# Gated cross attention with a routed feed-forward layer: queries kept on chip, gate on VectorE, new instruction orders

## The chip, the cores and the metric

The kernel runs on one core of one Trainium2 chip. The time is the device time of one execution in microseconds; lower is better. Before the change the median of three runs is 403.4 us (403.11 to 404.89).

## The reference, cut to what matters

`x` is 8 batches of 256 tokens of 256 features in float32, the context is 8 batches of 77 keys of 192 features, and there are 16 heads of 16 features.

```python
q = layernorm(x) @ wq + bq;  k = y @ wk + bk;  v = y @ wv + bv     # 16 heads of 16
attn = softmax(q k^T / sqrt(16))                                  # 256 x 77 per head and batch
x = x + tanh(g_xattn) * ((attn v) @ wo + bo)
z = layernorm(x)
top1 = argmax(softmax(z @ gate_w.T))                              # 2 experts
routed = sum over experts e of  relu(mask_e(z) @ w1[e] + b1[e]) @ w2[e] + b2[e]
shared = relu(z @ sw1 + sb1) @ sw2 + sb2                          # hidden size 1024
x = x + tanh(g_ffn) * (routed + shared)
```

The expert that a token did not choose sees a zero row, so it adds the constant row `relu(b1[e]) @ w2[e]`, called the other row below.

## The kernel before, in words

Most matrix products are made in float32r from a high and a low part of each operand: a helper `cut` issues three products (high·high, low·high, high·low). The attention values and the transposes are float32.

The work falls into a start (context turned, keys, values, first normalisation), attention over batches 0 to 7, the shared layer over five units (batches [0], [1,2], [3,4], [5,6], [7]) which is woven into the attention, and a routed loop over nine tiles of 256 sorted tokens. For the shared layer each unit has eight hidden chunks `h.u.c` and eight output chunks `y.u.c`. The gate and the counting of a unit (`ga`, `gt`, `ct`, then `ch`, `pl` on VectorE) give each token its slot; `scat` writes its row there by an indirect DMA, and the loop reads the sorted rows.

Every engine runs its own list of steps in a fixed order, written out as a string (`PE_ORDER`, `ACT_ORDER`, `DVE_ORDER`, `POOL_ORDER`, `SP_ORDER`, lines 73 to 139); semaphores join them. A step is `name.batch.part`. One batch of attention is: `nm` normalise (ScalarE), `in` turn the rows (TensorE), `ine`/`inl` cut them into high and low parts (ScalarE, VectorE), `qy` queries (TensorE), four quarters of scores `sc` (TensorE, L1452), each with maximum `sm`, subtraction `ss` and sum `su` (VectorE, L1144 to L1169), exponential `ex` (ScalarE) and division `di` (GpSimd, L672), then five turns `tn`, attend `va`, projection `ou` (TensorE) and the residual `x1` (VectorE).

From batch 1 on the queries go round through DRAM. ScalarE writes them twice, as float32 (`q32`) and rounded (`qe`, L849), GpSimd makes the low part (`ql`, L661), SyncE stores both parts (`qw`, L460) and loads them back as four pieces into `q_stack` (`qr`, L470), where one column block of 128 rows holds two heads four times. Keys go the same way (`kw`, `kr`, L434, L444: eight loads for each batch) and so do the values (`vw`, `vr`, L482, L496). All of these DMAs stand in SyncE's one list, and each of its waits holds back what stands behind it. Scores of one quarter are four products of 154 columns. All quarters use one pair of PSUM banks, `s_ps`, so quarter k+1 waits until VectorE has subtracted quarter k.

`LO_ON_POOL` (L71) names the hidden chunks whose low part GpSimd makes instead of VectorE. The gate is made of cut products on TensorE and turned back; the other rows are 48 products with a broadcast stationary operand (L1585).

## Time and profile before

| | |
|---|---|
| median of three runs | 403.4 us |
| the profiled execution | 406.97 us |
| its span, first to last instruction | 405.2 us |
| TensorE busy | 347.0 us (86%) |
| VectorE busy | 238.9 us (59%) |
| ScalarE busy | 211.7 us (52%) |
| GpSimd busy | 168.3 us (42%) |
| mean granted TensorE clock | 0.948 of full |

The span is what the trace covers; the execution's own time is 1.8 us longer. Busy shares are averages over stages that have different limits, so the windows below are cut where the first quarter of scores of each batch starts on TensorE: 31.44 us for batch 0, 53.23, 75.45, 103.60, 123.88, 143.90, 164.13 and 184.40 us for batches 1 to 7, and 286.48 us for the first product of the routed loop. In the names of operands, `q_parts`, `q_dram`, `q_stack` are the queries' round trip; `A<-B,C` is output and inputs.

### The profile page before, as it was taken

The page shows a single profiled execution, that of the slowest core. Times are in us where ns is not written, and L with a number is a line of the kernel's source. Part 1 is how long each engine was busy: PE and PEld are TensorE (multiplying, and loading weights), DVE is VectorE, ACT ScalarE, POOL GpSimd, SP SyncE. Part 2 cuts the span into 40 slices and gives each one's busy share as a digit, 9 for nine tenths or more (in the row PEclk, how much of TensorE's full clock was granted, in tenths as well). Part 3 has the DMA queues.
Part 4 walks back from the last instruction along what each step waited for, and adds up shares of the span by engine and source line. Part 5 has one row for each costly group of instructions (what it writes and reads, how often), then busy time and mean ns, then how long its engine had stood idle before and what let it go on. Part 6 is the DMA issues. An engine that isn't in the chain of part 4 may idle for free.

```text
span 405.2 us, 7324 instructions
## 1 busy us (share of the span) xinstructions
PE 347.0 (86%) x2411; PEld 317.5 (78%) x2411; DVE 238.9 (59%) x528; ACT 211.7 (52%) x430; POOL 168.3 (42%) x185
## 2 busy tenths in 40 slices
PE   1886637939799999999999999798799999999990
PEld 0664536828798889998899978688799999999990
DVE  4697639647689888787884248442244443444440
ACT  2538737244456667536485254633455566456450
POOL 9196825423162446232430118121234554544451
PEclk9999956978899999999999999899899999999995
DMA  6946898999979293703042011002202222111120
GB/s 183 326 107 141 208 302 208 284 236 169 214 138 200 79 205 110 141 11 106 21 144 98 2 52 54 0 26 79 79 7 73 78 78 68 42 48 42 62 78 26
DMA packets 49823, 45.82 MB, mean 113 GB/s; under 512 B 20942, under 2 KB 41973, under 8 KB 49797
## 3 DMA queue, kind: packets, MB, share of 16 engines
q1 hardware_dynamic: 46114, 37.90, 37.9%
q0 software_dynamic: 2784, 6.91, 5.4%
q10 hardware_dynamic: 899, 0.69, 0.6%
q8 instruction: 14, 0.23, 0.3%
q14 instruction: 12, 0.10, 0.1%
HBM read 29.98 MB, written 16.02 MB: 114 GB/s over the span
## 4 chain that ended last, share of the span: by engine, by line
PE 59%; DVE 12%; SPq 11%; DMA 8%; issue 4%; ACT 2%; POOL 1%; ACTq 1%; DVEq 0%; POOLq 0%
PE y_ps L1365 20%; PE h_ps L1365 15%; PE bank L1365 11%; PE s_ps L1365 9%; SPq L455 4%; DMA k_stack<-k_dram 2%; SPq L477 2%; SPq L493 2%; PE bank L1483 2%; DMA vec_rows<-in_L_ffn_gate_w 2%; DMA q_dram<-q_parts 2%; DVE nt L1049 2%; DVE rsum L1165 1%; DMA xs<-sorted_dram 1%; DVE probs L1159 1%
## 5 line engine op out<-in xcount | busy, mean ns | idle before, releaser
L676 POOL TENSOR_TENSOR probs<-probs,rinv 128x616 f32<-128x616 f32 x32 | 38.9, 1220 | 65.0 <-DVE rinv L1169 65.0
L1331 DVE TENSOR_TENSOR hT_lo<-h,hT_hi 128x256 fp32r<-128x256 f32 x72 | 33.6, 466 | 49.0 <-ACT h L1025 44.3
L1022 ACT ACTIVATE hT_hi<-h_ps,vec_cols 128x256 fp32r<-128x256 f32 x36 | 17.1, 476 | 47.3 <-PE h_ps L1365 43.9
L1365 PE MATMUL y_ps<-ew_hi,hT_hi 128*128 128x256 f32 x144 | 41.7, 289 | 0.0
L934 ACT ACTIVATE hT_hi<-h_ps,vec_cols 128x512 fp32r<-128x512 f32 (+1 forms) x40 | 24.1, 602 | 31.7 <-PE h_ps L1365 31.2
L1365 PE MATMUL y_ps<-ew_hi,hT_lo 128*128 128x256 f32 x144 | 40.5, 281 | 0.0
L1365 PE MATMUL y_ps<-ew_lo,hT_hi 128*128 128x256 f32 x144 | 40.5, 281 | 0.0
L1365 PE MATMUL bank<-pT,v_diag 128*128 128x256 f32 (+1 forms) x160 | 38.5, 397 | 0.3 <-DVE place_int L1231 0.3
L1365 PE MATMUL y_ps<-sw_hi,hT_hi 128*128 128x256 f32 x128 | 37.9, 296 | 0.9 <-DVE x_all L1259 0.9
L1483 PE MATMUL bank<-ident,probs 128*128 128x128 f32 (+1 forms) x160 | 24.9, 287 | 13.7 <-ACT q_parts L861 10.7
L1365 PE MATMUL y_ps<-sw_hi,hT_lo 128*128 128x256 f32 x128 | 36.1, 282 | 0.0
L1365 PE MATMUL y_ps<-sw_lo,hT_hi 128*128 128x256 f32 x128 | 36.1, 282 | 0.0
L1365 PEld LDWEIGHTS bank<-pT,v_diag 128*128 128x128 f32 (+1 forms) x160 | 31.5, 201 | 5.0 <-DVE place_int L1231 0.5
L766 POOL DMA_INDIRECT out<-final,scatter_token x18 | 20.3, 1125 | 34.5 <-issue 21.6
L1147 DVE TENSOR_REDUCE smax<-s_ps 128x8 f32<-128x616 f32 x32 | 24.9, 779 | 13.3 <-PE s_ps L1365 13.3
L1365 PE MATMUL h_ps<-x2T_hi,sw_hi 128*128 128x512 f32 (+1 forms) x80 | 30.1, 376 | 3.0 <-ACT h L939 3.0
L1483 PEld LDWEIGHTS bank<-ident,probs 128*128 128x128 f32 (+1 forms) x160 | 18.8, 144 | 17.0 <-ACT q_parts L861 11.6
L704 POOL TENSOR_TENSOR hT_lo<-h,hT_hi 128x512 fp32r<-128x512 f32 (+1 forms) x10 | 10.7, 1067 | 50.3 <-ACT h L939 50.3
L868 ACT ACTIVATE probs<-probs 128x616 f32<-128x616 f32 x32 | 23.0, 717 | 15.2 <-DVE probs L1159 15.2
L1165 DVE TENSOR_REDUCE rsum<-probs 128x8 f32<-128x616 f32 x32 | 25.2, 789 | 7.9 <-ACT probs L868 7.8
L1250 DVE TENSOR_TENSOR hT_lo<-h,hT_hi 128x512 fp32r<-128x512 f32 (+1 forms) x30 | 19.3, 647 | 16.9 <-ACT h L939 16.5
L1365 PE MATMUL h_ps<-x2T_lo,sw_hi 128*128 128x512 f32 (+1 forms) x80 | 28.4, 355 | 0.0
(186 smaller groups left out, 1107.6 us busy)
## 6 DMA issues: line engine op xcount, KB each, us to landing
q_stack<-q_dram SPq DMA_DIRECT2D x28, 256.0 KB, 5.6
v_diag<-v_rows SPq DMA_DIRECT2D x8, 512.0 KB
stage<-in_L_ffn_w SPq DMA_DIRECT2D x4, 1024.0 KB, 7.0
q_dram<-q_parts SPq DMA_DIRECT2D x7, 512.0 KB, 3.4
sorted_dram<-empty_rows SPq DMA_DIRECT2D x10, 257.0 KB, 10.7
xs<-sorted_dram SPq DMA_DIRECT2D x10, 257.0 KB
k_stack<-k_dram SPq DMA_DIRECT2D x56, 38.5 KB, 4.7
stage<-in_L_ffn_sw SPq DMA_DIRECT2D x2, 1024.0 KB, 9.1
```

The costliest lines, as they stand in the source:

```text
L455: sp.dma_start(k_stack[to, n, :, :, h, :].rearrange("r i g n -> r (i g) n").bitcast(F32), k_dram[h * HEAD_DIM:(h + 1) * HEAD_DIM, piece // ...
L676: nc.gpsimd.tensor_tensor(pq, pq, rinv[:, b % 2, k, :].unsqueeze(2).to_broadcast([P, HG, KEYS]), ALU.mult).then_inc(p_ready, 1)
L766: pool.indirect_dma_start(out=out[:, :], out_offset=bass.IndirectOffsetOnAxis(ap=scatter_token[:, t:t + 1], axis=0), in_=final[:, t, :], i ...
L868: nc.scalar.activation(probs[:, b % 2, k, :], probs[:, b % 2, k, :], ACT.Exp, scale=HEAD_DIM ** -0.5).then_inc(p_exp, 1)
L934: nc.scalar.activation(hT[0][:, q % HB, 0:width], h_ps[:, q % 2, 0:width], ACT.Relu, bias=b1_sb[:, 0, c:c + 1]).then_inc(h_hi, 1)
L1022: nc.scalar.activation(hT[0][:, c % HB, 0:RTOK], hidden_bank(c % 4)[:, 0:RTOK], ACT.Relu, bias=b1_sb[:, 1 + e, c:c + 1]).then_inc(h_hi, 1)
L1147: nc.vector.tensor_reduce(out=smax[:, b % 2, k, :].rearrange("p (n h) -> p n h", n=2), in_=score_heads(), axis=AX_X, op=ALU.max).then_inc( ...
L1165: nc.vector.tensor_reduce(out=rsum[:, b % 2, k, :], in_=probs[:, b % 2, k, :].rearrange("p (h k) -> p h k", k=KEYS), axis=AX_X, op=ALU.add ...
L1250: nc.vector.tensor_tensor(hT[1][:, q % HB, 0:width], h32[:, q % 2, 0:width], hT[0][:, q % HB, 0:width], ALU.subtract).then_inc(h_lo, 1)
L1331: nc.vector.tensor_tensor(hT[1][:, c % HB, 0:RTOK], h32[:, c % 2, 0:RTOK], hT[0][:, c % HB, 0:RTOK], ALU.subtract).then_inc(h_lo, 1)
L1365: return nc.tensor.matmul(out_, lhsT, rhs, start=start, stop=stop, **kw)
L1483: ins = nc.tensor.transpose(bank[m][0:ROWS[c], v * SEQ + t * P:v * SEQ + (t + 1) * P], probs[:, b % 2, g * TB + t, c * P:c * P + ROWS[c]], ...
```

## The change

- Queries no longer pass through DRAM. For each half of 64 rows (four heads) of a group, `q_stack` holds the high part in its own 64 rows and the low part in the other 64. ScalarE writes `q32` from PSUM and then copies the two halves (`qe`); GpSimd makes the low part in two instructions of 64 rows each, with a drain before and after each.
- Keys are laid out to match: `k_hi2` has the high part in both halves, over four heads, and `k_lo1` the low part. A batch takes 16 loads instead of 8, each of 16 rows with 4 or 2 pieces; the stores are 4 DMAs in place of 8 for each half of the batches. Scores of a quarter are four products of 308 columns, two over 128 rows and two over 64 rows.
- Quarters 0 to 7 (batches 0 and 1) alternate between `s_ps` and `h_ps`; values in the start go through `y_ps` instead of `h_ps`.
- The gate is one multiply with accumulation on VectorE per tile of 128 tokens; `ga`, `gt` and their ScalarE copies are gone. The other rows are eight multiply-adds on VectorE per expert and one float32 product with `ones`.
- Loads: the bias rows go on SyncE's queue right behind the first tile of x and the gate's row on GpSimd's; the big load of x waits for the second tile; the zero fill of the sorted rows (`fl`, ten DMAs) stands first in SyncE's list instead of behind the loads of batch 2. `k_hi2` is cleared on VectorE at its start.
- Statistics of batches 2 to 7 are taken batch by batch; `LO_ON_POOL` has five chunks of eight; the last weight split is on VectorE; the wait for the shared layer's last sum moves behind the first hidden products of the loop, and the loop's count is read on TensorE at `xst`. All five orders are new. `warm` issues nothing (`WARM = 0`).

```diff
@@ constants and orders (the order strings are cut)
-LO_ON_POOL = (0, 7)
+LO_ON_POOL = (2, 3, 4, 5, 7)
+WARM = 0
...
+    warm vt yt.0 yt.1 yt.2 yt.3 kp.0.0 kp.0.1 kp.1.0 in.0.0 kp.1.1 qy.0.1 vp.0 sc.0.0 sc.0.1 vp.1 in.1.0 vp.2
+    vp.3 sc.0.2 qy.1.1 sc.0.3 tn.0.0.0 tn.0.1.1 tn.0.2.0 tn.0.3.1 tn.0.4.0 in.2.1 sc.1.0 sc.1.1 qy.2.0 in.3.1
+    sc.1.2 sc.1.3 va.0.0 qy.3.1 sc.2.0 ou.0.0 in.4.1 sc.2.1 tn.1.0.0 tn.1.1.1 qy.4.0 tn.1.2.1 sc.2.2 tn.1.3.0
+    tn.1.4.1 in.5.0 sc.2.3 va.1.1 tn.2.0.0 sc.3.0 tn.2.1.0 ou.1.1 qy.5.0 sc.3.1 tn.2.2.1 tn.2.3.0 tn.2.4.1
...
+    fl vz kw.1 kw.0 wd.0 vw.0 kr.1 wd.1 vw.1 vr.0 kr.2 vw.2 vr.1 wd.2 kr.3 vw.3 vr.2 kr.4 vw.4 vr.3 wd.3 vw.5
+    vr.4 kr.5 vw.6 vr.5 kr.6 vw.7 ps.0 vr.6 kr.7 ps.1 vr.7 wd.4 wd.5 ps.2 xs ps.3 ps.4
...
-        q_stack = sb("q_stack", [P, 2, STACKS, GROUPS, SEQ], F32R, scope=att)
-        k_stack = sb("k_stack", [P, 2, STACKS, GROUPS, 2, KEYS], F32R, scope=att)
-        q_parts = sb("q_parts", [P, 2, GROUPS, SEQ], F32R, scope=att)
+        q_stack = sb("q_stack", [P, 2, GROUPS, 2, SEQ], F32R, scope=att)
+        k_hi2 = sb("k_hi2", [P, 2, 2 * GROUPS, HH, KEYS], F32R, scope=att)
+        k_lo1 = sb("k_lo1", [P, 2, GROUPS, HH, KEYS], F32R, scope=att)
         q32 = sb("q32", [P, GROUPS, SEQ], scope=att)
...
+        def score_banks(quarter):
+
+            return h_ps if quarter < 8 and quarter % 2 else s_ps
...
+            at = 0
+            for vec in (bq, bk, sb1, b1.rearrange("e h -> (e h)")):
+                n = vec.shape[0] // P
+                sp.dma_start(vec_rows[at:at + n, :], vec.rearrange("(n p) -> n p", p=P)).then_inc(vecs_in, 16)
+                at += n
...
+            sp.wait_ge(x_in[1], 16)
...
             def keys_in(b):
 
                 n = b % 2
-                if b == 1:
+                if b <= 2:
                     sp.wait_ge(cleared[0], 1)
+                    sp.wait_ge(cleared[1], 1)
                 else:
                     sp.wait_ge(s_ready, 4 * (b - 1))
-                sp.wait_ge(k_out[b // 4], 16 * 2 * STACKS)
-                for piece in range(4):
-                    for h in range(2):
-                        to = slice(piece * SR + h * HEAD_DIM, piece * SR + (h + 1) * HEAD_DIM)
-                        sp.dma_start(k_stack[to, n, :, :, h, :].rearrange("r i g n -> r (i g) n").bitcast(F32),
-                                     k_dram[h * HEAD_DIM:(h + 1) * HEAD_DIM, piece // 2, :, :,
-                                            b * KEYS:(b + 1) * KEYS].rearrange("r i g n -> r (i g) n")
+                sp.wait_ge(k_out[b // 4], 16 * 4)
+                cols = slice(b * KEYS, (b + 1) * KEYS)
+                for h in range(HH):
+                    rows = slice(h * HEAD_DIM, (h + 1) * HEAD_DIM)
+                    for m in range(2):
+                        to = slice(m * HR + h * HEAD_DIM, m * HR + (h + 1) * HEAD_DIM)
+                        sp.dma_start(k_hi2[to, n, :, h, :].bitcast(F32),
+                                     k_dram[0, :, rows, cols].rearrange("c r n -> r c n")).then_inc(k_in[n], 16)
+                        sp.dma_start(k_lo1[to, n, :, h, :].bitcast(F32),
+                                     k_dram[1, m * GROUPS:(m + 1) * GROUPS, rows, cols].rearrange("c r n -> r c n")
                                      ).then_inc(k_in[n], 16)
-
-            def queries_out(b):
-
-                sp.wait_ge(q_hi, b + 1)
-                sp.wait_ge(q_lo, b)
-                if b >= 3:
-                    sp.wait_ge(q_in[b % 2], 16 * 4 * ((b - 1) // 2))
-                sp.dma_start(q_dram[b % 2].rearrange("m p g s -> p m (g s)"),
-                             q_parts[:, :, :, :].rearrange("p m g s -> p m (g s)").bitcast(F32)
-                             ).then_inc(q_out[b % 2], 16)
-
-            def queries_in(b):
-
-                n = b % 2
-                if b >= 2:
-                    sp.wait_ge(s_ready, 4 * (b - 1))
-                sp.wait_ge(q_out[n], 16 * ((b + 1) // 2))
-                for piece in range(4):
-                    sp.dma_start(q_stack[piece * SR:(piece + 1) * SR, n, :, :, :].rearrange("r i g s -> r i (g s)"
-                                                                                            ).bitcast(F32),
-                                 q_dram[n, piece % 2].rearrange("(i r) g s -> r i (g s)", i=STACKS)
-                                 ).then_inc(q_in[n], 16)
...
             def queries_lo(b):
 
-                pool.wait_ge(q_32, b)
                 pool.wait_ge(q_hi, b + 1)
-                if b >= 2:
-                    pool.wait_ge(q_out[(b - 1) % 2], 16 * (b // 2))
-                nc.gpsimd.tensor_tensor(q_parts[:, 1, :, :].rearrange("p g s -> p (g s)"),
-                                        q32[:, :, :].rearrange("p g s -> p (g s)"),
-                                        q_parts[:, 0, :, :].rearrange("p g s -> p (g s)"), ALU.subtract
-                                        ).then_inc(q_lo, 1)
+                pool.drain()
+                for h in range(2):
+                    rows, other = slice(h * HR, (h + 1) * HR), slice((1 - h) * HR, (2 - h) * HR)
+                    ins = nc.gpsimd.tensor_tensor(q_stack[other, b % 2, :, h, :], q32[rows, :, :],
+                                                  q_stack[rows, b % 2, :, h, :], ALU.subtract)
+                    pool.drain()
+                ins.then_inc(q_lo, 1)
...
-                nc.gpsimd.tensor_tensor(lo, stage[:, n % 2, :], hi, ALU.subtract).then_inc(w_lo[n], 1)
+                for piece in range(4):
+                    cols = slice(piece * PTOK, (piece + 1) * PTOK)
+                    ins = nc.gpsimd.tensor_tensor(lo[:, cols], stage[:, n % 2, cols], hi[:, cols], ALU.subtract)
+                ins.then_inc(w_lo[n], 1)
...
+                ins.then_inc(q_32 if b else q_hi, 1)
+
+            def queries_hi(b):
+
+                act.wait_ge(q_32, b)
+                if b >= 3:
+                    act.wait_ge(s_ready, 4 * (b - 1))
+                for h in range(2):
+                    rows = slice(h * HR, (h + 1) * HR)
+                    ins = nc.scalar.activation(q_stack[rows, b % 2, :, h, :], q32[rows, :, :], ACT.Copy)
+                ins.then_inc(q_hi, 1)
...
+            def gate_difference():
+
+                dve.wait_ge(gate_in, 16)
+                nc.vector.tensor_tensor(gate_diff[:, :], gate_rows[:, 1, :], gate_rows[:, 0, :], ALU.subtract
+                                        ).then_inc(gate_cut, 1)
...
+            def other_sums(e, part):
+
+                n = 3 + 2 * e
+                w2_in = stage[:, n % 2, :].rearrange("p (c d) -> p c d", c=HC)
+                dve.wait_ge(w_in[n], 16)
+                dve.wait_ge(rb_cut, 1)
+                for c in range(part * HB, (part + 1) * HB):
+                    scale = relu_b1[:, e, c:c + 1]
+                    if c == 0:
+                        nc.vector.tensor_scalar(other_sum[:, e, :], w2_in[:, c, :], scale, None, ALU.mult
+                                                ).then_inc(other_step[e], 1)
+                        continue
+                    dve.wait_ge(other_step[e], c)
+                    nc.vector.scalar_tensor_tensor(out=other_sum[:, e, :], in0=w2_in[:, c, :], scalar=scale,
+                                                   in1=other_sum[:, e, :], op0=ALU.mult, op1=ALU.add
+                                                   ).then_inc(other_step[e], 1)
...
+                dve.wait_ge(gate_cut, 1)
+                dve.wait_ge(xn2_ready, u + 1)
+                for t in range(tiles):
+                    ins = nc.vector.scalar_tensor_tensor(
+                        out=gate_term[:, t, :], in0=xn2[:, u % 2, t, 0:DIM], scalar=1.0, in1=gate_diff[:, :], op0=ALU.mult,
+                        op1=ALU.mult, accum_out=gate_sb[:, t:t + 1])
+                ins.then_inc(gate_rdy, 1)
...
-                        pe.wait_ge(q_in[b % 2], 16 * 4 * ((b + 1) // 2))
-                        pe.wait_ge(k_in[b % 2], 16 * 8 * ((b + 1) // 2))
-                    for i in range(STACKS):
-                        ins = mm(s_ps[:, i // 2, i % 2 * SK:(i % 2 + 1) * SK],
-                                 q_stack[:, b % 2, i, g, t * P:(t + 1) * P],
-                                 k_stack[:, b % 2, i, g, :, :].rearrange("p h k -> p (h k)"), True, True)
+                        pe.wait_ge(q_lo, b)
+                        pe.wait_ge(k_in[b % 2], 16 * 16 * ((b + 1) // 2))
+                    tokens = slice(t * P, (t + 1) * P)
+                    for half in range(2):
+                        mm(s_to[:, half, 0:HALF], q_stack[:, b % 2, g, half, tokens],
+                           k_hi2[:, b % 2, half * GROUPS + g, :, :].rearrange("p h k -> p (h k)"), True, False)
+                    for half in range(2):
+                        rows = slice(half * HR, (half + 1) * HR)
+                        ins = mm(s_to[:, half, 0:HALF], q_stack[rows, b % 2, g, half, tokens],
...
+            def other(m):
+
+                fill_bank(m, other_scaled, 1)
+                pe.wait_ge(iotas, 8)
+                for e in range(EXPERTS):
+                    pe.wait_ge(other_step[e], HC)
+                    ins = mm(bank[m][:, e * DIM:(e + 1) * DIM], ones[:, :], other_sum[:, e, :], True, True)
...
+                    pe.wait_ge(seam_rdy, 1)
+                    tiles_of_0 = pe.value_load(tiles0_int[0:1, 0:1], min_val=1, max_val=RTILES - 1)
...
-            pe.wait_ge(y_out, len(UNITS))
```

## Rows read from the trace of the kernel before

**Rows 1.** Ten windows; us, then busy us per engine, PEclk, DMA share, GB/s.

```profile
0.00:31.44 31.44, 19.27 (x86) 13.72 (x86) 22.34 (x74) 12.33 (x27) 21.33 (x42) 1.00 0.71 204
31.44:53.23 21.79, 12.32 (x72) 9.19 (x73) 13.05 (x27) 14.42 (x30) 15.57 (x18) 0.98 0.78 185
53.23:75.45 22.22, 15.85 (x68) 13.86 (x69) 14.88 (x18) 11.86 (x20) 10.88 (x9) 0.64 0.93 272
75.45:103.60 28.15, 17.94 (x114) 15.78 (x112) 19.47 (x45) 11.87 (x24) 7.01 (x7) 0.88 0.99 197
103.60:123.88 20.28, 20.28 (x141) 19.38 (x141) 14.98 (x27) 12.10 (x26) 8.24 (x8) 0.92 0.88 211
123.88:143.90 20.02, 18.90 (x129) 16.38 (x128) 17.36 (x42) 12.79 (x26) 6.84 (x6) 1.00 0.53 118
143.90:164.13 20.23, 20.23 (x131) 18.16 (x130) 16.73 (x33) 12.74 (x23) 10.74 (x11) 1.00 0.74 163
164.13:184.40 20.27, 19.82 (x143) 18.48 (x141) 15.33 (x37) 11.26 (x20) 5.65 (x5) 1.00 0.36 80
184.40:286.48 102.08, 94.33 (x644) 85.04 (x642) 56.61 (x120) 51.14 (x87) 29.35 (x27) 0.98 0.16 55
286.48:405.20 118.72, 108.02 (x900) 107.53 (x900) 48.17 (x108) 61.24 (x153) 52.70 (x54) 0.95 0.20 56
```

**Rows 2.** Groups by line, ScalarE: busy us, mean ns, idle before and its releaser.

```profile
L861 ACT ACTIVATE q_parts<-bank,vec_cols 128x256 fp32r<-128x256 f32 x14 | 5.8, 470 | 13.2 <-DMA q_dram<-q_parts 13.2
```

**Rows 3.** Timeline of SyncE's queue, 0 to 110 us.

```profile
49.66 7.00 SPq L493 DMA_DIRECT2D v_rows<-v  x2
...
88.82 8.30 SPq L455 DMA_DIRECT2D k_stack<-k_dram  x8
...
106.43 3.69 SPq L455 DMA_DIRECT2D k_stack<-k_dram  x8
```

**Rows 4.** Timeline of TensorE: scores, other products, one attend step.

```profile
98.12 0.57 PE L1365 MATMUL s_ps<-k_stack,q_stack 128*128 128x154 f32 x4
98.53 0.28 PE L1365 MATMUL bank<-x2T_hi,gw_hi 128*2 128x256 f32 x1
...
219.79 4.49 PE L1365 MATMUL bank<-pT,v_diag 128*128 128x256 f32 x20
```

**Rows 5.** The chain that ended last: start, us, what.

```profile
150.10 0.87 PE bank L1483 x8
...
204.18 1.39 PE h_ps L1365 x6
...
207.01 1.44 PE y_ps L1365 x12
```

**Rows 6.** Groups by line, VectorE, shapes apart.

```profile
L1159 DVE TENSOR_TENSOR probs<-s_ps,smax 128x616 f32<-128x616 f32 x32 | 25.3, 791 | 1.4
L1165 DVE TENSOR_REDUCE rsum<-probs 128x8 f32<-128x616 f32 x32 | 25.2, 789 | 7.9 <-ACT probs L868 7.8
L1250 DVE TENSOR_TENSOR hT_lo<-h,hT_hi 128x512 fp32r<-128x512 f32 x18 | 12.2, 685 | 9.5 <-ACT h L939 9.4
...
L1049 DVE TENSOR_TENSOR nt<-nt,rstd 128x2 f32<-128x2 f32 x12 | 6.3, 528 | 0.4
...
L1049 DVE TENSOR_TENSOR nt<-nt,rstd 128x4 f32<-128x4 f32 x9 | 1.5, 164 | 0.3
```

**Rows 7.** Groups by line, GpSimd, shapes apart.

```profile
L667 POOL TENSOR_TENSOR q_parts<-q,q_parts 128x512 fp32r<-128x512 f32 x7 | 11.0, 1574 | 13.4 <-ACT q_parts L861 12.4 <-issue 1.0
L704 POOL TENSOR_TENSOR hT_lo<-h,hT_hi 128x512 fp32r<-128x512 f32 x6 | 7.7, 1290 | 31.6 <-ACT h L939 31.6
```

**Rows 8.** Timeline of TensorE, start of the kernel.

```profile
11.46 0.28 PE L1397 MATMUL bank<-ident,vec_rows 32*128 32x32 f32 x1 [3.62 <-DMA vec_rows<-in_L_ffn_gate_w]
...
13.02 4.44 PE L1365 MATMUL h_ps<-pT,stage 96*128 96x308 f32 x8
```

**Rows 9.** Timeline of TensorE, first routed product.

```profile
286.48 0.38 PE L1365 MATMUL h_ps<-xsT_hi,ew_hi 128*128 x1 [2.49 <-issue]
```

329 lines of the change are left out of this document (134 added, 195 removed).

## Prediction, made before the changed kernel ran

> **What bounds the kernel now.** I read the windows first, because the busy shares of the page average over stages with different limits. The reader is to see three stages [rows 1]. From the first scores of batch 3 at 103.60 us on, TensorE is busy for nearly all of each window (20.28 of 20.28, 18.90 of 20.02, 20.23 of 20.23, 19.82 of 20.27 us) and a batch takes 20.0 to 20.3 us. Ahead of that, batches 0 to 2 take 21.8, 22.2 and 28.2 us while TensorE is busy for 12.3, 15.9 and 17.9, VectorE for 13.1, 14.9 and 19.5, and the granted clock is down to 0.64 and 0.88. The DMA engines are at 0.78, 0.93 and 0.99 there. So the early batches wait for transfers. The last window, 118.72 us, is the routed loop, bound by TensorE, and the change leaves its products alone.
>
> Then I asked which transfer. ScalarE stands idle for 13.2 us ahead of the rounded queries, all of it for the store of the queries [rows 2]. On SyncE's queue the issues themselves are slow in that stretch: eight key loads take 8.30 us at 88.82 and only 3.69 us at 106.43, and two value stores took 7.00 us [rows 3]. One queue, full, serves queries, keys, values, fill and weights.
>
> **Prices.** TensorE's steps go by the distance between starts at full clock: four 154-column scores 0.41 us (98.12 to 98.53) and an attend step 4.3 us (4.49 less the tail of the last product) [rows 4]; eight turns of 128x128 0.87, so 0.45 for a step of four; six 512-column products 1.39 (a hidden chunk `h`, or a gate, of a big unit) and twelve of 256 columns 1.44 (`y`, `qy`, `ou`) [rows 5]. The small units' `h` and `y` cost half. VectorE: 0.8 for each of a quarter's passes, the sum with its reciprocal 0.95; 0.6 for the low part of a 512-wide tile [rows 6]; 1.5 for a residual with statistics, 0.2 for each of the 13 steps of a root. For each interval between the first scores of two batches I add the steps that the order strings put there.
>
> Before, the larger of TensorE's and VectorE's sums for the seven intervals is 11.3, 15.5, 19.4, 17.9, 17.9, 20.0, 19.4 us. The measured ones are 21.8, 22.2, 28.2, 20.3, 20.0, 20.2, 20.3 [rows 1]. The excess is 10.5, 6.7, 8.8 in the stretch of full queues and 2.4, 2.1, 0.2, 0.9 behind it. This check says that where transfers don't interfere, such a sum is right within 2.4 us.
>
> **Part by part.**
> *Scores.* Four products of 308 columns in place of 154. The trace has no float32r product of 308 columns; by the spacing of 256 columns, 0.12 us [rows 5], it is 0.12 x 308/256 = 0.143, so 0.57 for a quarter against 0.41. 28 quarters: +4.5 us of TensorE. Bounds: 0 (if rows of 64 or the write of fewer pieces pay back) and twice that.
> *Gate and other rows.* The gates leave TensorE: 3 x 1.39 + 2 x 0.7 + 1.4 for the small turns = -7.0 us. The other rows: 48 x 0.12 = 5.8 goes, two float32 products of about 0.42 (an attend step has ten for 4.3) come: -4.9. With the scores TensorE is 7.4 us lighter. VectorE pays: 16 multiplies with accumulation and 16 multiply-adds of 256 columns, no row shows them; the nearest, the 512-wide subtraction at 0.685 and the 12-row root steps at 0.17, bound one at 0.17 and 0.69. I take 0.38, the half of 0.69 and a little, so +12 us. 15 hidden chunks, 9 of them 512 wide, move from VectorE (-8 us there) to GpSimd, at 1.29 for a wide one [rows 7].
> *Queries.* The round trip's 35 DMAs on SyncE go; by their shapes they move 1.5 MB a batch. The eight extra key loads of a batch cost 8 x 0.46 = 3.7 us at the price of the quiet queue and 8.3 at that of the full one [rows 3]. I take the quiet one: a batch then costs SyncE 16 x 0.46 for keys and about 2 for values, some 10 us, under the 12 to 25 us that the engines need. GpSimd's low part becomes two instructions; 1.57 was one [rows 7], so 1.3 to 1.6 more a batch with its drains, and it is made a batch ahead of its scores. Cover for it is the 12 us of the batch in front; without it each batch would start 3 us late.
> *Start.* The first scores stood at 31.4 us. The keys wait for the bias rows, which land at 11.3 us, last of all on ScalarE's queue [rows 8]; and the low part of the first input stood behind the 12-tile statistics on VectorE. Both go. From the context at 6.6 us TensorE has turns 2.5, three keys 4.4 + 1.3 and one more 1.3, the input 0.6, queries 1.5: 18.2, and 0.8 for their copy: 19. I take 20; 24 if the bias rows land as late as before, since `vt` now stands first on TensorE. The store of the zeros, the fill and the big load of x now come together here; their cover is the work of batch 0, 21 us of VectorE, and the keys of batch 1 should land at 42 to 44.
> *Batches.* In the new orders TensorE's sums for the seven intervals are 14.4, 9.9, 13.1, 14.0, 21.0, 25.0, 22.5 and VectorE's 20.9, 11.9, 14.7, 18.8, 19.7, 24.0, 17.8. For instance batch 1 on TensorE: 4 x 0.57, two queries 2.86, an input 0.45, an attend 4.3. The larger ones add to 134.8. I add 2 us of excess to each of the first four and 3.2 to the last three: 146.0. Bounds: 134.8, and 166 with all of the old excess kept.
> *Behind the last batch's first scores.* Before: 90.5 us of steps in 102.1 measured. Now 79.4 of steps. The 2.49 us in front of the loop [rows 9] go with the wait for the last sum and the count that is read earlier, all but about 0.5; the rest of the excess stays: 79.4 + 11.6 - 2.0 = 89.0. Bounds: 84 and 94. The new wait, for the seam ahead of `xst`, has eight outputs and five hidden chunks of the last units queued behind it; VectorE's seam stands some 10 us ahead.
> *Loop:* 118.7, unchanged.
>
> **Sum.** 20 + 146.0 + 89.0 + 118.7 = 373.7 us of span, against 405.2. The profiled execution took 406.97, 1.8 more than its span and 3.6 more than the median of 403.4. So the forecast is 373.7 + 1.8 - 3.6 = 371.9, say 372 us, 31 less than before. Of the 31, 11 come from the start, 7 from the intervals of the batches (153.0 to 146.0, although they hold more of the shared layer than before), 13 from what is left behind them.
>
> **A rule that speaks against it.** VectorE's two-column root product took 528 ns on average but the four-column one 164 ns [rows 6]: something held the small ones. The Trainium skill, page "SBUF — State Buffer", section "SBUF: two separate sides", says that a VectorE instruction with two SBUF inputs and a GpSimd instruction that reads SBUF exclude each other for a whole instruction. That agrees in direction with these rows; by the four-column row alone nothing is lost. The new gate and other-row instructions all have two SBUF inputs while GpSimd gets more work; the price is in the second rival.
>
> **Rivals.**
> 1. *The excess vanishes* (shorter queues, every stage at its sum): 19 + 134.8 + 84 + 118.7 = 356.5, time 355. For it: the last three windows before. Against it: two engines share the load evenly in the early intervals. 0.17.
> 2. *VectorE becomes the bound by waiting for GpSimd.* 18 of its new instructions lie ahead of batch 7's scores. If each waits for one of 1.29 us [rows 7] that is 23 us on VectorE, whose sums are equal to TensorE's: 373.7 + 23 = 397, time 395. Against it: windows with GpSimd at 10.7 of 20 us busy held 20.2 us. 0.10.
> 3. *The change doesn't free the queues.* Keys, values, fill and weights keep them full and the old excess stays: 373.7 + 20 = 394, time 392. Against it: 1.5 MB a batch go. 0.12.
> 4. *Slower: SyncE's queue with the doubled key loads.* 16 loads at 1.04 us (8.30/8) are 16.6, value stores 7.0 [rows 3], value loads, two issues too, at half of that 3.5: 27.1 us a batch. From batch 1 at 44, batch 7 would start at 207, and the end is 207 + 89 + 118.7 = 415, time 413. It decides from (405.2 - 118.7 - 89 - 44)/6 = 25.6 us a batch on. Against it: those prices were paid beside the queries. 0.05.
>
> **How the numbers follow.** The forecast has 0.56 with a range of its own of 362 to 384. With rivals 1 and 3 the range is 354 to 394; the rest, and half of rival 2, is under 2 in 10. Within 0.5% (2 us) is what a measurement of this kernel can't tell from no change. Rivals 1 to 3 and the forecast are all faster: 0.93 with a little off for chains of several; same 0.02; slower 0.05.
>
> **What would show it.** First scores near 20 us; those of batch 1 at 42 to 44 and of batch 7 near 166; the loop's first product near 255; DMA share under 0.7 from 40 to 105 us; key loads near 0.46 us to issue; a quarter's four products 0.57 us apart. Wrong if SyncE's key issues stay near 1 us each, or if the new VectorE instructions take far more than 0.4 us, or if TensorE waits for GpSimd's low parts of the hidden chunks.

## The result, and the profile after

The changed kernel takes 375.41 us (median of 4 runs, 374.7 to 377.67), the kernel before 403.28 beside it; the ratio is 0.931 with an interval of 0.926 to 0.936. The forecast was 372 us with a range of its own of 362 to 384. The profiled execution took 376.05 us for a span of 374.3. Times are medians of all executions; two of the six of `both_late` fell in a slower state, without which its median is 380.7.

The windows of the kernel after, cut at the same places of the work as [rows 1] (first scores of each batch, first routed product); columns as there:

```profile
0.00:22.79 22.79, 13.59 (x57) 10.07 (x58) 13.63 (x45) 9.98 (x22) 14.93 (x35) 1.00 0.93 252
22.79:51.12 28.33, 16.27 (x81) 12.03 (x80) 21.91 (x52) 13.32 (x23) 14.22 (x17) 0.77 0.80 220
51.12:65.34 14.22, 14.00 (x67) 11.48 (x65) 10.59 (x17) 10.99 (x19) 11.23 (x14) 0.75 0.61 141
65.34:81.35 16.01, 14.85 (x94) 11.88 (x93) 14.39 (x23) 12.46 (x24) 11.38 (x11) 1.00 0.45 113
81.35:98.95 17.60, 15.79 (x103) 12.93 (x101) 16.31 (x41) 11.11 (x20) 9.44 (x10) 1.00 0.61 153
98.95:121.41 22.46, 22.45 (x160) 20.39 (x161) 19.84 (x51) 14.68 (x32) 11.54 (x12) 1.00 0.19 43
121.41:147.94 26.53, 26.53 (x168) 23.06 (x168) 23.84 (x67) 16.48 (x29) 15.28 (x16) 1.00 0.32 78
147.94:172.11 24.17, 23.91 (x158) 20.67 (x156) 19.87 (x38) 15.00 (x27) 15.45 (x15) 1.00 0.14 46
172.11:258.58 86.47, 82.06 (x547) 74.25 (x546) 56.89 (x118) 47.25 (x78) 33.89 (x31) 1.00 0.17 58
258.58:374.30 115.72, 105.64 (x902) 105.44 (x900) 48.74 (x109) 61.93 (x153) 52.60 (x55) 0.98 0.21 59
```

The reader is to see where the waiting was and where it is. The stretch of full queues is gone: in [rows 1] the DMA share stood at 0.78 to 0.99 over four windows, here it is 0.61 or less from 51 us on. The 31 us of span divide into 8.7 from the start (31.4 to 22.8), 3.7 from the seven intervals (153.0 to 149.3, with more of the shared layer in them), 15.6 behind the last batch's first scores (102.1 to 86.5) and 3.0 from the loop. The trace of before is of an execution 3.6 us over its median, and this bears on the second share: in the trace of experiment 10, an execution of 400.07 us whose code is the same up to batch 7, the seven intervals take 149.4 us. So the 3.7 us from the intervals can be scatter. One window is longer than before: the first interval, 28.3 us against 21.8.

The pieces that bear out or contradict a price. First TensorE after; start, us, then what, its shapes, how many, and the idle time with its releaser:

```profile
8.32 0.28 PE L1392 MATMUL bank<-ident,vec_rows 28*128 28x28 f32 x1 [8.32 <-DMA vec_rows<-in_L_ffn_b]
11.22 1.36 PE L1360 MATMUL h_ps<-v_diag,stage 96*128 96x308 f32 x2 [0.41 <-ACT v_diag L779]
...
46.71 2.87 PE L1486 MATMUL bank<-ident,probs 128*104 128x128 f32 x12 [10.02 <-POOL probs L666]
...
121.41 0.53 PE L1360 MATMUL s_ps<-k_hi,q_stack 128*128 128x308 f32 x2
121.87 0.41 PE L1360 MATMUL s_ps<-k_lo,q_stack 64*128 64x308 f32 x2
122.21 0.38 PE L1360 MATMUL h_ps<-x2T_hi,sw_hi 128*128 128x256 f32 x1
```

Then SyncE's queue after, where one of the sixteen key loads of a batch stands for all (from 19.68 to 26.7 us the queue stores the zeros):

```profile
10.00 9.56 SPq L522 DMA_DIRECT2D sorted_dram<-empty_rows  x10
...
26.75 6.04 SPq L447 DMA_DIRECT2D k_dram<-probs  x8
32.90 0.53 SPq L514 DMA_DIRECT2D stage<-in_L_ffn_sw  x1
...
54.71 0.43 SPq L464 DMA_DIRECT2D k_hi<-k_dram  x1
```

And groups by line, VectorE and GpSimd, shapes apart:

```profile
L1188 DVE SCALAR_TENSOR_TENSOR gate_term<-xn,gate_diff 128x256 f32<-128x256 f32 x16 | 12.6, 837 | 3.4 <-ACT xn L893 3.4
L1118 DVE SCALAR_TENSOR_TENSOR other_sum<-stage,relu_b,other_sum 128x256 f32<-128x256 f32 x14 | 8.2, 589 | 0.6
L1114 DVE TENSOR_SCALAR other_sum<-stage,relu_b 128x256 f32<-128x256 f32 x2 | 0.7, 350 | 2.0 <-DMA stage<-in_L_ffn_w 2.0
L657 POOL TENSOR_TENSOR q_stack<-q,q_stack 64x512 fp32r<-64x512 f32 x14 | 17.8, 1274 | 10.8 <-ACT q_stack L858 9.7 <-issue 0.2
L694 POOL TENSOR_TENSOR hT_lo<-h,hT_hi 128x512 fp32r<-128x512 f32 x15 | 20.8, 1404 | 10.9 <-ACT h L916 10.7
```

Most key loads issue in 0.41 to 0.43 us. A quarter's four score products cost TensorE 0.80 us here (121.41 to 122.21). Over the quarters of batches 1 to 7 that distance is 0.71 in nine and 0.80 to 0.98 in fifteen of 28, where [rows 4] had 0.41; the last four, 1.13 us and more, hold a stretch of low clock or a wait. Sixteen quarters, those of batches 4 to 7, can be compared at full clock: their mean is 0.79 us in this trace and 0.48 in that of before. The 16 gate multiplies average 0.84 us because one of them took 5.98 and one 1.51; the others take 0.42. Of the 14 multiply-adds of the other rows two took 1.59 and 0.84, the others 0.48 to 0.49. Each of these four long ones ran beside a low part on GpSimd.

The long first interval is read from the chain that ended last; start, us, what:

```profile
32.90 7.60 DMA stage<-in_L_ffn_sw
...
40.52 1.91 ACT sw_hi L926
42.43 0.61 ACT probs L864
...
43.07 0.81 DVE rsum L1150
...
44.18 2.40 POOL probs L666 x2
...
46.71 1.94 PE bank L1486 x8
```

The fill holds SyncE for 9.6 us, the stores of zeros and keys for 13, and only then is the shared expert's first weight load issued. It lands at 40.5. ScalarE's split of it stands between two exponentials, and the sum, the scaling and TensorE's turns follow it: that is TensorE's wait of 10.02 us.

How much of it belongs to this one execution can be read from experiments 6 and 9. Up to batch 4 they run the same instructions in the same order as the change, and up to batch 7 all but the gate's operation in experiment 9. TensorE's wait is shorter there, as in this line of experiment 6:

```profile
44.09 2.87 PE L1486 MATMUL bank<-ident,probs 128*104 128x128 f32 x12 [7.25 <-POOL probs L666]
```

Their first scores of batch 1 stand at 48.2 and 49.0 us (51.1 in the change), those of batch 4 at 97.4 and 98.4 (99.0), and those of batch 7 at 172.0 and 173.0 (172.1). The first interval is 26.2 and 26.5 us instead of 28.3. So where a start of an early batch is compared with the change below, 2 to 3 us are scatter.

### The profile page after: what moved, and what is told of

Read it like the earlier page. It is cut to its first block, busy times and chain, and to the rows that moved or that the text cites. A ratio compares the mean times of both kernels' runs of the same rounds, so it can differ in the third digit from the quotient of the medians.

```text
span 374.3 us, 7206 instructions
## 1 busy us (share of the span) xinstructions
PE 335.1 (90%) x2321; PEld 302.2 (81%) x2321; DVE 246.0 (66%) x560; ACT 213.2 (57%) x420; POOL 190.0 (51%) x207
## 4 chain that ended last, share of the span: by engine, by line
PE 59%; DVE 15%; SPq 7%; issue 6%; DMA 5%; ACT 3%; POOL 3%; POOLq 1%; DVEq 0%; ACTq 0%
PE y_ps L1360 21%; PE h_ps L1360 13%; PE s_ps L1360 10%; PE bank L1360 9%; PE bank L1486 3%; SPq L522 2%; DVE ew_lo L1259 2%; DMA stage<-in_L_ffn_sw 2%; DMA stage<-in_L_ffn_w 2%; DMA x_all<-in_x 2%; DVE smax L1132 2%; DVE probs L1144 2%; SPq L447 2%; DVE other_sum L1118 2%; SPq L436 1%
## 5 line engine op out<-in xcount | busy, mean ns | idle before, releaser
L694 POOL TENSOR_TENSOR hT_lo<-h,hT_hi 128x512 fp32r<-128x512 f32 (+1 forms) x25 | 28.5, 1149 | 25.7 <-ACT h L916 25.6
L1360 PE MATMUL bank<-pT,v_diag 128*128 128x256 f32 (+1 forms) x160 | 36.4, 382 | 0.7 <-DVE x_all L1168 0.7
L911 ACT ACTIVATE hT_hi<-h_ps,vec_cols 128x512 fp32r<-128x512 f32 (+1 forms) x40 | 24.2, 605 | 20.3 <-PE h_ps L1360 19.8
L1486 PE MATMUL bank<-ident,probs 128*128 128x128 f32 (+1 forms) x160 | 24.5, 289 | 12.5 <-POOL probs L666 11.2
L685 POOL DMA_INDIRECT sorted_dram<-xn,place_int x16 | 18.1, 1131 | 33.1 <-DVE place_int L1222 28.0
L1360 PEld LDWEIGHTS bank<-pT,v_diag 128*128 128x128 f32 (+1 forms) x160 | 29.8, 190 | 5.4 <-DVE x_all L1168 0.9
L864 ACT ACTIVATE probs<-probs 128x616 f32<-128x616 f32 x32 | 22.9, 716 | 19.7 <-DVE probs L1144 19.5
L1150 DVE TENSOR_REDUCE rsum<-probs 128x8 f32<-128x616 f32 x32 | 25.2, 787 | 9.5 <-ACT probs L864 9.4
L872 ACT ACTIVATE pT<-bank 128x512 f32<-128x512 f32 x40 | 23.0, 595 | 12.5 <-PE bank L1486 12.2
```

The costliest lines, as they stand in the source:

```text
L685: pool.indirect_dma_start(out=sorted_dram[:, :], out_offset=bass.IndirectOffsetOnAxis(ap=place_int[:, n, t:t + 1], axis=0), in_=xn2[:, n, ...
L694: nc.gpsimd.tensor_tensor(hT[1][:, q % HB, 0:width], h32[:, q % 2, 0:width], hT[0][:, q % HB, 0:width], ALU.subtract).then_inc(h_lo_pool, 1)
L864: nc.scalar.activation(probs[:, b % 2, k, :], probs[:, b % 2, k, :], ACT.Exp, scale=HEAD_DIM ** -0.5).then_inc(p_exp, 1)
L872: nc.scalar.activation(pT[:, 2 * u:2 * u + 2, :].rearrange("p c s -> p (c s)"), bank[m][:, :], ACT.Copy).then_inc(pT_sb, 1)
L911: nc.scalar.activation(hT[0][:, q % HB, 0:width], h_ps[:, q % 2, 0:width], ACT.Relu, bias=b1_sb[:, 0, c:c + 1]).then_inc(h_hi, 1)
L1150: nc.vector.tensor_reduce(out=rsum[:, b % 2, k, :], in_=probs[:, b % 2, k, :].rearrange("p (h k) -> p h k", k=KEYS), axis=AX_X, op=ALU.add ...
```

## The experiments

Each ratio is to the kernel before, with its interval; the changed kernel has 0.931 by its own comparison. "First scores" are read on TensorE as above.

**1. The fill behind batch 2's key loads** (`fill_late`).

```diff
-    fl vz kw.1 kw.0 wd.0 vw.0 kr.1 wd.1 vw.1 vr.0 kr.2 vw.2 vr.1 ...
+    vz kw.1 kw.0 wd.0 vw.0 kr.1 wd.1 vw.1 vr.0 kr.2 fl vw.2 vr.1 ...
```

> The changed kernel with the zero fill of the sorted rows (ten DMAs, 9.6 us of SyncE's queue from 10.0 us on) moved behind the key loads of batch 2. Theory: the 5.4 us by which the interval from the first scores of batch 0 to those of batch 1 is longer than forecast come from one chain on SyncE's queue: fill, zeros, key stores, weights load (lands at 40.5), ScalarE's weight split at 40.5 to 42.4, the third exponential behind it. Without the fill in front the load is issued some 5 us earlier, so batch 1 starts near 46 instead of 51.1 and the time falls by 4 to 6 us, to about 370. Rival 1, the keys of batch 1 and not the weights are the limit: the keys too come 5 us earlier, same gain, told apart by weights_split_late. Rival 2, the fill costs as much wherever it stands (it delays the loads of batch 3): 375, no change.

382.12 us, 0.950 (0.947 to 0.954): slower than the change, which none of the three forecasts had. Batch 1's first scores stand at 46.7 us, 4.4 earlier (1.5 to 2.3 against experiments 6 and 9), but batch 4's at 102.3, 3.4 later. The longest wait of TensorE in between stands between batches 3 and 4, as its timeline shows:

```profile
100.70 1.11 PE L1518 MATMUL bank<-ident,xn 128*128 128x128 f32 x4 [5.28 <-DVE oT_lo L1159]
```

and VectorE's timeline says what it was doing:

```profile
94.61 0.35 DVE L1114 TENSOR_SCALAR other_sum<-stage,relu_b 128x256 f32<-128x256 f32 x1 [3.42 <-DMA stage<-in_L_ffn_w]
95.00 3.29 DVE L1118 SCALAR_TENSOR_TENSOR other_sum<-stage,relu_b,other_sum 128x256 f32<-128x256 f32 x3
```

The first half of the other-row sums reads a weight load directly. In this order the load comes late, and the values' low part, the root and the batch's normalisation queue behind it.

**2. ScalarE's split of the weights behind the last turned copy of batch 0** (`weights_split_late`).

```diff
-    ... q32.1.1 qe.1 wh.0 ex.0.2 te.0.0.0 ... nm.2 te.0.4.0 nm.3
+    ... q32.1.1 qe.1 ex.0.2 te.0.0.0 ... nm.2 te.0.4.0 wh.0 nm.3
```

> The changed kernel with ScalarE's split of the first shared weights moved behind the last turn copy of batch 0, nothing else. Theory: ScalarE's 4.9 us wait for the load no longer stands between exponentials 1 and 2 of batch 0; TensorE's wait of 10.0 us for GpSimd's divisions falls to about 5. Batch 1's keys are issued until 46.3 and land near 48, so the first scores of batch 1 come at 48 to 49 instead of 51.1: time down 2 to 3 us, to about 373. Rival, the keys' landing alone decides batch 1: no change beyond 1 us. Rival 2, the late split delays hidden chunk 0: nothing at all or slower.

376.53 us, 0.939 (0.935 to 0.944). Batch 1 starts at 47.8 us, 3.3 earlier than in the change but only 0.4 and 1.2 earlier than in experiments 6 and 9; as intervals, 25.3 us against 28.3, 26.2 and 26.5. So the split costs 1 to 3 us. But batch 2 starts at 64.6, only 0.8 earlier than the change's 65.3 (and later than the 61.5 and 62.3 of experiments 6 and 9): VectorE's low part of the same weights stands ahead of its maxima and now waits for the late split. Nothing is left at the end.

**3. Both moves** (`both_late`): the diffs of 1 and 2 together.

> Both moves together. Theory (two chains in one place, each hides part of the other): more than either, 6 to 8 us less than the changed kernel, about 368. Rival, both act on one chain and the fill alone takes all: the same as fill_late within 1 us.

382.28 us, 0.950 (0.946 to 0.953). Batch 1 at 47.2 us, batch 4 at 100.1. By the median it is `fill_late` again, but its runs scatter from 378.5 to 385.8, and the trace is of the fastest; the two can't be told apart by their times.

**4. Those orders with the sums moved.** `fill_late_sums_later` is `fill_late` with one more edit, and `three_moves` and `four_moves` take it up:

```diff
-    ... inl.6.0 ss.3.2 ot.0.0 ro.0.8 ...   ... inl.7.0 sm.4.1 ot.0.1 ss.4.1
+    ... inl.6.0 ss.3.2 ro.0.8 ...          ... inl.7.0 sm.4.1 ot.0.0 ot.0.1 ss.4.1
```

> fill_late again (the filling of the slots behind batch 2's key loads), with one more move: VectorE's first half of the other-row sums of the first unit (four operations on a weight load) stands behind batch 4's second scores instead of behind batch 3's third. Theory: in fill_late that load lands late, and VectorE waits for it 3.4 us at 94.6 us, with the roots, the normalised batch and the value parts behind it. Then this run gets back most of the 6.7 us that fill_late cost against the change: 375 to 378 us, and the sums no longer wait. Rival: fill_late loses its time in the queues themselves, whose transfers of batches 3 and 4 run beside the filling; then it stays at 380 to 383 us.

378.93 us, 0.943 (0.939 to 0.948). The wait on the load is gone and batch 4 starts at 98.6 us, 3.7 earlier than in `fill_late` and as early as in the change. Then up to 2.9 us are lost before batch 5 (25.3 us against 22.5 in the change and 23.9 in experiments 6 and 9). The timelines of VectorE and TensorE:

```profile
107.48 0.79 DVE L1132 TENSOR_REDUCE smax<-s_ps 128x8 f32<-128x616 f32 x1
108.19 0.34 DVE L1114 TENSOR_SCALAR other_sum<-stage,relu_b 128x256 f32<-128x256 f32 x1
108.57 4.11 DVE L1118 SCALAR_TENSOR_TENSOR other_sum<-stage,relu_b,other_sum 128x256 f32<-128x256 f32 x7
112.59 0.80 DVE L1144 TENSOR_TENSOR probs<-s_ps,smax 128x616 f32<-128x616 f32 x1
```
```profile
113.44 0.55 PE L1360 MATMUL s_ps<-k_hi,q_stack 128*128 128x308 f32 x2 [1.81 <-DVE probs L1144]
```

Eight sums now stand between a maximum and its subtraction, where the change has four, and the next scores wait for that subtraction. So the theory holds for the wait (all of the 3.7 us), and the move has a price of its own. The time, 378.9 us, lies between the two forecasts.

`three_moves` takes that edit and two others to the change; `four_moves` also moves the fill behind `wd.3` on SyncE's queue:

```diff
-    ... q32.1.1 qe.1 wh.0 ex.0.2 ... te.0.4.0 nm.3           (ScalarE)
+    ... q32.1.1 qe.1 ex.0.2 ... te.0.4.0 wh.0 nm.3
-    ... r1.2.12 wl.0 sm.1.0 ... val.0.0 su.1.3 sm.2.0 ...     (VectorE)
+    ... r1.2.12 sm.1.0 ... val.0.0 su.1.3 wl.0 sm.2.0 ...
```

> The same with the filling left at the head of SyncE's queue. Theory: batch 1 at 47.5 to 48.5 us as in weights_split_late, and batch 2 now as much earlier (62 instead of 64.6), since VectorE's maxima no longer wait for the late split: 373 to 375 us. Rival: 375 to 377 us, as weights_split_late.

> The change with four steps moved: the filling behind the first unit's second weight load on SyncE's queue; ScalarE's first split of the shared expert's weights behind batch 0's attended rows; VectorE's low part of it behind batch 1's last sums; VectorE's first other-row sums behind batch 4's second scores. Theory (the excess of the first interval is the filling, then the weights that stand between the exponentials; each needs the cover behind it moved too): first scores of batch 1 at 45 to 47 us (51.1 in the change), half of it kept until the loop: 370 to 373 us. Rival: every stretch up to the loop is set by VectorE's and TensorE's own work and what is won early is lost in the next intervals, as in the two moves made alone: 375 to 378 us.

`three_moves` took 380.57 us (0.945, 0.940 to 0.949), `four_moves` 380.62 (0.945, 0.940 to 0.950); both theories and both rivals forecast too little. Batch 1 starts at 48.0 us in both, 3.1 us earlier than in the change, batch 5 at 128.8 and 126.3, 7.4 and 4.9 later. Both take 4.3 us longer than the change between batches 4 and 5 (2.9 longer than experiments 6 and 9), where the moved sums alone cost `fill_late_sums_later` 2.9 (1.4). The rest goes before that: TensorE's second scores of batch 2 wait 3.26 and 2.01 us for VectorE's subtraction, since the low part of the weights (2.3 us) has to stand somewhere too. What is won at 48 us is not carried to the loop by any of these orders.

**5. One pair of banks for the first scores** (`one_bank_pair`).

```diff
-            return h_ps if quarter < 8 and quarter % 2 else s_ps
+            return s_ps
```
(with the waits that belong to it, and one maximum of batch 1 behind a subtraction)

> The changed kernel with all scores in s_ps: quarters 0 to 7 no longer alternate with h_ps, each waits for the subtraction of the one before (VectorE's maximum of quarter 3 of batch 1 stands one place later for it). Theory: batch 0 is bound by the weights wait, so its alternation is hidden; batch 1's quarters lose about 1 us each at most: 375 to 377. Rival, the second pair is what made the early batches short: four waits of 1.7 us as in the kernel before, 380 or more.

388.55 us, 0.965 (0.961 to 0.968), 13 us above the change. A wait of its TensorE, which the change has once, for 0.5 us; us in total, times, longest:

```profile
PE s_ps L1360 <- DVE probs L1144: 13.0, 6, 5.6
```

My theory fell. The rival's time held, though it had four waits of 1.7 us and there are six of up to 5.6: in this schedule the second pair is worth 13 us. The first scores of batches 0 and 2 stand at 21.4 and 73.8 us, 9.9 further apart than in the change (22.8 and 65.3) and 12.6 to 12.9 further than in experiments 6 and 9, and these are the batches that have the pair.

**6. The old way into the loop** (`loop_entry_old`): the waits for all sums and the reading of the tile count stand before the first routed product again.

```diff
+            pe.wait_ge(y_out, len(UNITS))
             pe.wait_ge(h_32, CHUNKS_SHARED)
+            pe.wait_ge(seam_rdy, 1)
+            tiles_of_0 = pe.value_load(tiles0_int[0:1, 0:1], ...)
```

> The changed kernel with the entry of the routed loop as before: TensorE waits for the shared layer's last sum and reads the count in front of the loop. Theory: the gap of 2.5 us in front of the first routed product comes back and the granted clock is down behind it, as it was before (0.69 over the first 5.5 us of the loop), which costs 1 to 2 us more; 375.4 + 4 = 379 to 380, and the loop takes about 118 us instead of 115.7. Rival, the gap alone: 377.9, with the clock at 1.00. Rival 2, the wait is covered: no change.

376.95 us, 0.939 (0.935 to 0.943): 1.5 us over the change, near the first rival, whose clock it has too. The gap is back, 2.52 us with nothing shown as its releaser, but the clock behind it is not. The first 6 us of the loop of this kernel, of the one after and of the one before; us, busy us of PE, PEld, DVE, ACT, POOL, then PEclk, DMA share, GB/s:

```profile
260.00:266.00 6.00, 6.00 (x51) 6.00 (x52) 2.21 (x6) 3.96 (x11) 2.08 (x2) 1.00 0.23 69
```
```profile
258.58:264.58 6.00, 6.00 (x54) 6.00 (x53) 2.96 (x7) 4.04 (x11) 1.54 (x2) 1.00 0.32 90
```
```profile
286.48:292.48 6.00, 6.00 (x38) 6.00 (x39) 1.78 (x5) 3.31 (x8) 2.08 (x2) 0.72 0.23 68
```

Before, the loop begins at a granted clock of 0.72 and gets through 38 products; after, at 1.00, through 54. In the kernel before the fall comes behind the gap: 1.00 until 286.48 us, then 0.94, 0.50 and 0.69 in the next three windows of some 2 us. It is not particular to one execution, for experiments 7 and 10, whose entry is that of before, have 0.72 and 38 products as well. Sixteen products at 0.12 us are 1.9 of the 3.0 us by which the loop is shorter. An idle gap of 2.5 us alone doesn't bring the lower clock. The traces differ in what comes ahead of it: in the three with the lower clock TensorE had also waited 0.88 us some 12 to 13 us before the first routed product, in this variant it had no wait in the 25 us ahead. Whether that decides it stays open.

**7. The kernel before with an eighth of its query traffic** (`before_eighth_queries`).

```diff
-                sp.dma_start(q_dram[b % 2]..., q_parts[:, :, :, :]...
+                sp.dma_start(q_dram[b % 2][:, 0:SR, 0, :]..., q_parts[0:SR, :, 0, :]...
-                    sp.dma_start(q_stack[piece * SR:(piece + 1) * SR, n, :, :, :]..., q_dram[n, piece % 2]...
+                    sp.dma_start(q_stack[piece * SR:(piece + 1) * SR, n, 0, 0, :]..., q_dram[n, piece % 2][0:SR, 0, :]
```

> The kernel before, with the stores and loads of the queries cut to an eighth of their rows and columns (the same 35 DMAs and the same waits; the rest of the queries' tile is zero, set once at the start). It leaves out most of the queries, so its scores are of other values, the same work. Theory, the volume of the round trip fills the DMA queues and so slows the issues of the keys and values: the intervals of batches 0 to 2 fall from 72 us together to 50 to 55, the time from 403 to 383 to 388. Rival, the order of SyncE's list with its waits and landings is the limit, not the volume: at most 5 us are gained, 398 or more.

395.21 us, 0.983 (0.979 to 0.987): 6.6 us faster than the 401.8 beside it. Its windows from the first scores of batch 0 to those of batch 3:

```profile
32.89:50.49 17.60, 12.07 (x72) 9.16 (x73) 13.04 (x27) 12.70 (x27) 13.50 (x16) 1.00 0.61 133
50.49:70.55 20.06, 14.90 (x71) 13.00 (x70) 14.88 (x18) 13.68 (x24) 12.10 (x11) 0.74 0.80 237
70.55:94.54 23.99, 18.59 (x113) 16.24 (x111) 16.94 (x39) 11.45 (x23) 7.71 (x8) 0.86 0.84 186
```

61.7 us against 72.2 of [rows 1], 70.1 in the trace of experiment 10 (the same code there) and 58.6 of the change. So the bytes of the queries account for 8.4 to 10.5 us of these intervals, and 6.6 reach the end; the start is 1.5 us later than in [rows 1], which takes some of it back. Neither theory is right by itself: the round trip with its waits and issues, kept here, still holds ScalarE and TensorE.

**8. Key loads in halves, 32 a batch** (`keys_twice`).

```diff
-                for h in range(HH):
-                    rows = slice(h * HEAD_DIM, (h + 1) * HEAD_DIM)
+                half = HEAD_DIM // 2
+                for h, r in ((h, r) for h in range(HH) for r in range(2)):
+                    rows = slice(h * HEAD_DIM + r * half, h * HEAD_DIM + (r + 1) * half)
```

> The changed kernel with each key load split into two of 8 rows: 32 loads for a batch, the same bytes. Theory: issues stay at 0.46 us each, so a batch costs SyncE some 17 us. That is more than the intervals of batches 1 to 3 (14 to 17.6) and the first load stands directly in front of batch 1's scores: batch 1 starts 7 us later, batches 2 and 3 lose 2 or 3 more, and the later ones (22 us and more) hide it: 384 to 388. Rival (the fourth of the prediction), issues slow down to 1 us each when there are more: 395 or more. Rival 2, the loads have slack: 376.

386.54 us, 0.961 (0.957 to 0.965): 11 us slower than the change. Each load of 8 rows issues in 0.30 us, so a batch costs SyncE 11.1 us in place of 7.4. Batch 1 is not later (50.2 us), batch 2 is 4.3 us later and batch 4 10 us. First ScalarE ahead of batch 2, then SyncE's queue, VectorE and TensorE ahead of batch 4:

```profile
56.23 0.59 ACT L816 ACTIVATE v<-y_ps 77x512 f32<-77x512 f32 x1 [4.97 <-DMA v_rows<-v]
```
```profile
94.48 2.10 SPq L515 DMA_DIRECT2D stage<-in_L_ffn_w  x1
```
```profile
102.15 0.35 DVE L1115 TENSOR_SCALAR other_sum<-stage,relu_b 128x256 f32<-128x256 f32 x1 [4.71 <-DMA stage<-in_L_ffn_w]
```
```profile
107.43 1.11 PE L1519 MATMUL bank<-ident,xn 128*128 128x128 f32 x4 [6.11 <-DVE oT_lo L1160]
```

What is late is what stands behind the keys in the queue. The first is a store of values: it is issued at 49.6 us (46.9 in the change), ScalarE's next copy of values waits 4.97 us for it (1.12 in the change), and the weight split and the exponentials of batch 1 stand behind that copy. The second is a weight load, issued at 94.5 us (86.1 in the change): again the other-row sums wait for it with the whole batch behind them. The time lies in my theory's range, but not by its path, which had batch 1 late by its keys: that is luck. The fourth rival had the right queue and the wrong customers.

**9. A gate operation with one SBUF input** (`gate_one_input`).

```diff
-    scalar_tensor_tensor(out=gate_term, in0=xn2, scalar=1.0, in1=gate_diff, op0=mult, op1=mult, accum_out=gate_sb)
+    tensor_reduce(out=gate_sb, in_=xn2, axis=X, op=add)
```

> The changed kernel with the gate's multiply replaced by a plain sum over the same 256 columns, one operand from on-chip memory instead of two. It leaves the gate's weights out, so tokens go to other experts; the loop has the same nine tiles. Theory: one of the 16 gate instructions took 5.98 us because four of GpSimd's ran beside it, and this is hidden under TensorE: all 16 sums take 0.45 us or less, and the time stays at 375 within 1.5 us. Rival, VectorE is a bound and what it waits for GpSimd costs time: 370 or less. Rival 2, the wait has nothing to do with the second operand: a sum of several us remains.

376.47 us, 0.936 (0.932 to 0.941). First the timelines of VectorE and GpSimd of the change around its one slow multiply, then those of this run:

```profile
231.87 5.98 DVE L1188 SCALAR_TENSOR_TENSOR gate_term<-xn,gate_diff 128x256 f32<-128x256 f32 x1 [1.23 <-ACT xn L893]
```
```profile
232.54 5.02 POOL L694 TENSOR_TENSOR hT_lo<-h,hT_hi 128x512 fp32r<-128x512 f32 x4
```
```profile
231.62 0.75 DVE L1188 TENSOR_REDUCE gate_sb<-xn 128x1 f32<-128x256 f32 x2 [1.23 <-ACT xn L893]
232.40 4.93 DVE L1193 TENSOR_SCALAR chosen<-gate_sb 128x2 f32<-128x2 f32 x1
```
```profile
232.29 5.00 POOL L694 TENSOR_TENSOR hT_lo<-h,hT_hi 128x512 fp32r<-128x512 f32 x4
```

All sixteen gate sums now take 0.41 to 0.42 us, and the block of 4.9 us sits on the next instruction instead, for just as long as GpSimd makes four low parts in a row. The two sums in front of it had ended by the time GpSimd's work was under way (232.37 and 232.29 us), so they don't test whether a sum is held. VectorE's passes over the scores test it better: all 32 maxima and all 32 sums of a quarter in the change, operations with one input, take 0.75 to 0.80 us, and 46 of the 64 met an instruction on GpSimd.

Time is unchanged within its scatter, but this run still has the block and can't price it. In the change TensorE waits only 0.18 us for the counting behind the block. Its longer wait inside the block is for GpSimd itself, which the prediction had named as a sign of being wrong:

```profile
233.87 0.39 PE L1360 MATMUL y_ps<-sw_hi,hT_hi 128*128 128x256 f32 x1 [1.50 <-POOL hT_lo L694]
```

**10. One of eight chunks of the other rows, in the kernel before** (`before_one_other_chunk`).

```diff
-                for c in range(HC):
+                for c in range(1):
```

> The kernel before with the other row of each expert taken over one of its eight chunks (it leaves the other seven out): 42 products fewer on TensorE in its span behind batch 7. The prediction took this work at about 5 us of TensorE's time there. Theory: 397 to 399.5 us. Rival: TensorE waits for VectorE in that stretch and the products fit into its gaps: 401 to 404 us.

400.69 us, 0.998 (0.994 to 1.002). By the time alone, 1.8 us less, neither theory is decided. The window behind batch 7's first scores, which answers to the ninth of [rows 1]:

```profile
180.61:279.36 98.75, 89.52 (x602) 79.94 (x600) 56.62 (x120) 50.87 (x87) 29.32 (x27) 0.98 0.17 57
```

It holds 42 products fewer and 4.8 us less of TensorE, and is 3.3 us shorter. In the trace of experiment 7, whose code there is that of before, the stretch takes 100.4 us with 92.7 of TensorE, and against it this one has 3.2 us less of TensorE and is 1.6 shorter. So between a half and two thirds of the work removed there show in the stretch.

## Why the prediction was right

**The start.** Forecast 20 us, measured 22.8. The queries' biases no longer wait for the gate's rows, but TensorE still waits for the last of the bias rows until 8.32 us (11.46 in [rows 8]), and the keys begin at 11.2 instead of 13.0. The bound of 24 was for this. Experiments 6 and 9, with the same instructions there, start at 22.0 and 22.5 us, so under one of the 2.8 us is scatter of the execution.

**The intervals.** Sum 146.0 forecast, 149.3 measured; one by one 22.9, 13.9, 16.7, 20.8, 23.1, 25.2, 23.4 against 28.3, 14.2, 16.0, 17.6, 22.5, 26.5, 24.2. The last three are within 1.3 us each. The miss is the first, by 5.4 us: I said that the fill, the zeros and the load of x have the work of batch 0 for cover, and I watched the keys of batch 1. They were issued by 46.3 us, and the scores at 51.1 don't wait for them. I did not count that a weight load stands behind the same stores and that ScalarE's split of it stands between the exponentials. Of the 5.4 us some 2 are scatter, since the same instructions take 26.2 and 26.5 us in experiments 6 and 9. Moving the split (experiment 2) takes 1 to 3 us away, moving the fill (experiment 1) 1 to 3 as well (25.4 us). But neither got the time back at the end, nor did any of the orders of experiment 4. The scatter shows the same without any change of order: experiments 6 and 9 start batch 1 2 to 3 us earlier than the change and batch 7 at the same time within 1 us. So the first interval is longer than forecast, and yet not what limits this schedule. The interval from batch 3 to 4 is 3.2 us shorter than forecast in the change but 19.8 us, 1.0 shorter, in the other two; the sum of the intervals, 149.3, 150.0 and 150.5 us in the three traces, is steadier than its parts.

**The scores.** This term was mis-sized. I took 0.57 us a quarter with an upper bound of twice the growth, 0.73; measured are 0.71 at the least and 0.80 and more in most. By the sixteen quarters that can be compared at full clock it is 0.31 more than before, 8.8 us over 28 quarters where the sum had 4.5; the bound of twice that held. The trace also shows where it goes. The two 64-row products run side by side: each lasts 0.41 us, and both together 0.41. In the quickest quarters the second 128-row product starts 0.14 us after the first, as I had priced it, the two 64-row ones another 0.23 later, and the next step 0.34 after them. So 0.09 us are lost where 128 rows give way to 64, and the pair costs 0.05 more than two products at my price. The sum held all the same, and by luck, because the excess that I had added beside it was not needed in full: in the last three intervals TensorE's 68.5 plus 12 x 0.23 is 71.3, of 73.2 measured, where I had put 3.2 us of excess.

**Gate and other rows.** The gate multiply was taken at 0.38 us and starts 0.35 apart; the other-row step was taken at 0.38, starts 0.52 apart and took 0.59 on average. Together with the blocks, 21.5 us instead of 12 on VectorE. What I missed is an order: the first operation of each expert's other row reads a weight load directly, at the head of VectorE's queue. In the change the second of them waits 2.0 us, and TensorE waits 0.68 us for the residual behind it. In experiments 6 and 9, in the change's own order, the first waits 1.1 us, and TensorE 2.6 us behind it in experiment 6: this order stands at the edge. In experiments 1 and 8 the wait is 3.4 and 4.7 us, and batch 4 is late by it.

**The second rival** priced VectorE's waiting for GpSimd at 1.29 us an instruction, 23 us in all. The mechanism exists and is rarer: four of the 32 new instructions were held, for 5.6, 1.1, 1.1 and 0.4 us, and only one of 1.1 and that of 0.4 lie in the stretch ahead of batch 7 for which the rival had 23 us. The Trainium skill ("SBUF — State Buffer", section "SBUF: two separate sides") gave the direction; experiment 9 agrees that a VectorE instruction is held while GpSimd's low parts run (4.93 against 5.00 us). The maxima and sums with one input agree too, for none was held. The experiment also shows an instruction of one tensor and constants, `chosen`, held for the same time. That section names VectorE's two-port modes as a second case beside two inputs; no run here shows in which mode `chosen` ran.

**Queries.** The forecast gave 7 us to the intervals for the freed queues. Experiment 7 shows 6.6 us in the kernel before by the bytes alone. As a difference of intervals the 7 us aren't shown: it is 3.7 us between the two traces and 0.1 against experiment 10's. The DMA share is under 0.7 from 51 us on (0.80 in the window ahead of that, where I had said from 40). Key loads start 0.46 to 0.47 us apart, which is the quiet price, so the third and fourth rivals are out.

**The banks** had no term in the sum. I let the intervals stand at the engines' own sums, which assumes that scores don't wait for the pass before; experiment 5 shows that this assumption is what the second pair buys, 13 us. The gains of experiments 5 and 7 were measured in different kernels and can't be added. No run takes back the new start, or the new orders as a whole; what they bring is read from windows alone.

**Behind batch 7** 89.0 was forecast and 86.5 measured: TensorE idles 4.4 us there against 7.8 before. **The loop** was said to be unchanged and is 3.0 us shorter, 1.9 of them by the clock at its head. These two hide the 2.8 and 3.3 us that start and intervals cost more: 373.7 forecast, 374.3 measured, with four terms each off by about 3. That the span came out within 1 us is luck; that each term stayed inside its bounds is not, save the loop's, which had none. The time, 375.4 us against 371.9, is off by more than the span, because the forecast took off 3.6 us by which the profiled execution of before was over its median, and after the change this difference is 0.6.

## What to carry to other kernels

Sums of steps by stage forecast a saturated stretch within some 5%, but where a stretch is not saturated, walk the queue behind every store that is moved forward and ask which instruction of which engine reads the last of it. When work moves from a busy engine to another, look at its operands: an operation that reads a load directly puts that load's arrival at the head of its new engine's queue. An idle gap seen early is worth its length only if the engines behind it have room; six orders that started batch 1 earlier by 3 to 4.5 us than the change ended no sooner. And before a difference of 3 us between two traces is explained, look for a run with the same instructions there: here such runs differ by 2 to 3 us in the early batches.

## What the runs showed of the hardware

A 64-row product of 308 columns took 0.41 us where the 128-row one took 0.31, but two 64-row products on the two halves of the rows ran side by side, 0.41 us together. Two of each took 0.71 to 0.98 us from their start to the next step's in 24 of 28 quarters. A key load issues in 0.42 us with 16 rows and in 0.30 with 8. GpSimd's back-to-back low parts held a VectorE instruction for their whole run, 5 us for four, in two traces; 64 maxima and sums with one input, 46 of them beside GpSimd, were never held. And a gap of 2.5 us in front of the loop was followed by a granted clock of 0.72 in the kernel before and of 1.00 in a variant of the one after.
